# The order of the matmuls within a tile of an expert layer on one core: three whole passes in place of three products at each piece of weights

## The reference

```python
shared = jax.nn.silu(flat @ shared_gate_w) * (flat @ shared_up_w) @ shared_down_w
xs = flat[sorted_tok]                                # the two best of 16 experts for each token
g = jax.lax.ragged_dot(xs, gate_w, group_sizes)      # 1024 -> 512 per expert
u = jax.lax.ragged_dot(xs, up_w, group_sizes)        # 1024 -> 512
h = jax.nn.silu(g) * u
dn = jax.lax.ragged_dot(h, down_w, group_sizes)      # 512 -> 1024
routed = jnp.zeros_like(flat).at[sorted_tok].add(sorted_w[:, None] * dn)
output = (shared + routed).reshape(b, s, d)
```

## Time and profile before

| what | value |
|---|---|
| time, median of 3 runs | 3263.84 us (3263.45 to 3267.43) |
| the profiled execution's own time | 3260.97 us |
| its span, from first to last instruction | 3259.4 us |
| mean granted clock of TensorE | 0.974 |
| TensorE busy with matmuls | 3012.4 us, 92% |
| ScalarE, VectorE busy | 1025.7 us (31%), 1681.5 us (52%) |

### The profile page before, as it was taken

How to read it: one execution, slowest core, us unless ns; L and a number is a source line. 1 busy time by engine, 2 the same in 40 slices (tenths; PEclk the granted TensorE clock), 3 DMA queues, 4 the chain that set the end, 5 groups by cost and what they waited for, 6 DMA issues and landing times.

```text
span 3259.4 us, 50815 instructions
## 1 busy us (share of the span) xinstructions
PE 3012.4 (92%) x17478; PEld 2478.7 (76%) x17479; DVE 1681.5 (52%) x3164; ACT 1025.7 (31%) x1940; POOL 609.4 (19%) x572
## 2 busy tenths in 40 slices
PE   3799998898989998689999999999999999999998
PEld 3677777777777776578888888888888888888886
DVE  3687777787878775323333333333333334444444
ACT  3444443343444331223233333333333321111110
POOL 1233333333333432100000000000000001111111
PEclk9699999999999997799999999999999999999999
DMA  4333333333434321553333442443242234444444
GB/s 151 117 105 121 115 119 116 105 105 107 126 108 123 111 85 46 216 179 140 135 136 135 142 173 103 174 161 114 101 175 100 109 135 152 145 154 137 157 146 133
DMA packets 200706, 424.54 MB, mean 130 GB/s; under 512 B 85472, under 2 KB 85984, under 8 KB 200160
## 3 DMA queue, kind: packets, MB, share of 16 engines
q1 hardware_dynamic: 176160, 349.67, 31.8%
q0 software_dynamic: 24400, 72.96, 6.8%
HBM read 333.42 MB, written 102.27 MB: 134 GB/s over the span
## 4 chain that ended last, share of the span: by engine, by line
PE 54%; DMA 1%; DVE 1%; issue 1%; ACT 1%; SPq 1%; ACTq 0%; POOL 0%; POOLq 0%; DVEq 0%
PE p_g_b L1451 17%; PE p_up_b L1451 17%; PE p_y_b L1439 16%; PE p_x_b L1419 3%; PE p_h_b L1426 1%; DMA mid_y<-y_b 1%; DVE w_lo_b L1294 1%; ACT w_hi_b L1237 1%; SPq L1139 0%; DMA xg_b<-mid_xn,idx_b 0%; DMA r_b<-mid_y,slot_now_b 0%; ACTq L1103 0%; DMA idx_b<-mid_lists 0%; SPq L1138 0%; DVE r_b L1347 0%
## 5 line engine op out<-in xcount | busy, mean ns | idle before, releaser
L1310 DVE TENSOR_TENSOR ht_lo_b<-p_h_b,ht_hi_b 128x512 fp32r<-128x512 f32 x105 | 72.5, 691 | 557.4 <-ACT ht_hi_b L1249 553.4
L1451 PE MATMUL p_g_b<-w_hi_b,xt_hi_b 128*128 128x512 f32 x840 | 339.2, 404 | 20.3 <-DVE w_lo_b L1294 18.4
L1439 PE MATMUL p_y_b<-w_hi_b,ht_hi_b 128*128 128x512 f32 x840 | 336.9, 401 | 6.8 <-DVE ht_lo_b L1310 6.8
L1451 PE MATMUL p_g_b<-w_hi_b,xt_lo_b 128*128 128x512 f32 x840 | 328.9, 391 | 0.0
L1451 PE MATMUL p_up_b<-w_lo_b,xt_hi_b 128*128 128x512 f32 x840 | 328.7, 391 | 0.0
L1451 PE MATMUL p_up_b<-w_hi_b,xt_lo_b 128*128 128x512 f32 x840 | 328.5, 391 | 0.0
L1439 PE MATMUL p_y_b<-w_hi_b,ht_lo_b 128*128 128x512 f32 x840 | 328.1, 391 | 0.0
L1451 PE MATMUL p_up_b<-w_hi_b,xt_hi_b 128*128 128x512 f32 x840 | 328.0, 391 | 0.0
L1439 PE MATMUL p_y_b<-w_lo_b,ht_hi_b 128*128 128x512 f32 x840 | 327.9, 390 | 0.0
L1451 PE MATMUL p_g_b<-w_lo_b,xt_hi_b 128*128 128x512 f32 x840 | 326.8, 389 | 0.0
L1322 DVE SCALAR_TENSOR_TENSOR sg_b<-th_b,p_g_b 128x512 f32<-128x512 f32 x105 | 72.2, 687 | 486.6 <-ACT th_b L1279 486.6
(11 more groups left out here) (216 smaller groups left out, 5837.5 us busy)
## 6 DMA issues: line engine op xcount, KB each, us to landing
mid_y<-y_b SPq DMA_DIRECT2D x73, 512.0 KB, 3.3
x<-in_x SPq DMA_DIRECT2D x64, 512.0 KB, 3.7
gbd<-mid_g_row SPq DMA_DIRECT2D x64, 512.0 KB, 5.1
stage_b<-in_eg SPq DMA_DIRECT2D x16, 2048.0 KB
stage_b<-in_eu SPq DMA_DIRECT2D x16, 2048.0 KB, 15.2
stage_b<-in_ed SPq DMA_DIRECT2D x16, 2048.0 KB, 19.4
ctx_t<-in_ctx_t SPq DMA_DIRECT2D x32, 512.0 KB, 4.6
ctx_v<-in_ctx SPq DMA_DIRECT2D x32, 512.0 KB, 7.7
```

Source lines behind the costliest of these rows:

```text
L1310: nc.vector.tensor_tensor(ht_lo[:, :, :], p_h[:, :, :], ht_hi[:, :, :].bitcast(f32), ALU.subtract).then_inc(ht_rdy, 1)
L1439: last = nc.tensor.matmul(p_y[n][:, :], a[:, k, :], b[:, GUP + k, w], start=(k == 0 and m == 0), stop=(k == FE // P - 1 and m == 2))
L1451: mm = nc.tensor.matmul(out[:, :], a[:, k, :], w[:, k, o:o + FE], start=(k == 0 and m == 0), stop=(k == KD - 1 and m == 2))
```

## The change

In `body` and in `down` on TensorE, the loop over the three products is now outside of the loop over the pieces. A tile makes all its high by high products, then all low by high, then all high by low. Each pass waits only for the parts that it reads: the first for `xt_hi` (`xt_hi_rdy`) and `w_hi` (`gu_hi`), the second for `xt_lo` (`xt_rdy`) and `w_hi`, the third for `w_lo` (`gu_split`). In `down` likewise `d_hi` twice and `d_split`. `turn_h` is called behind piece 3 of the second pass. No other engine's program is changed.

```diff
-            trio = ((xt_hi, w_hi), (xt_lo, w_hi), (xt_hi, w_lo))
+            trio = ((xt_hi, w_hi, xt_hi_rdy, gu_hi), (xt_lo, w_hi, xt_rdy, gu_hi), (xt_hi, w_lo, xt_rdy, gu_split))
...
                 for n in range(2):
-                    for k in range(FE // P):
-                        if n == 0:
-                            pe.wait_ge(d_split, (PIECES - GUP) * e + (k + 1))
-                        w = slice(512 * n, 512 * n + 512)
-                        for m, (a, b) in enumerate(((ht_hi, w_hi), (ht_lo, w_hi), (ht_hi, w_lo))):
+                    w = slice(512 * n, 512 * n + 512)
+                    for m, (a, b, w_part) in enumerate(((ht_hi, w_hi, d_hi), (ht_lo, w_hi, d_hi), (ht_hi, w_lo, d_split))):
+                        for k in range(FE // P):
+                            if n == 0:
+                                pe.wait_ge(w_part, (PIECES - GUP) * e + (k + 1))
                             last = nc.tensor.matmul(p_y[n][:, :], a[:, k, :], b[:, GUP + k, w],
                                                     start=(k == 0 and m == 0), stop=(k == FE // P - 1 and m == 2))
                     last.then_inc(y_ps, 1)
 
             def body(i, q, e, c, first, prev, last):
                 ge(pe, h_rdy, i)
-                for k in range(KD):
-                    if k % 4 == 0:
-                        pe.wait_ge(xt_rdy, 2 * i + (k // 4 + 1))
-                    pe.wait_ge(gu_split, GUP * e + (k + 1))
-                    for m, (a, w) in enumerate(trio):
+                for m, (a, w, x_part, w_part) in enumerate(trio):
+                    for k in range(KD):
+                        if k % 4 == 0:
+                            pe.wait_ge(x_part, 2 * i + (k // 4 + 1))
+                        pe.wait_ge(w_part, GUP * e + (k + 1))
                         for out, o in ((p_g, 0), (p_up, FE)):
                             mm = nc.tensor.matmul(out[:, :], a[:, k, :], w[:, k, o:o + FE],
                                                   start=(k == 0 and m == 0), stop=(k == KD - 1 and m == 2))
-                    if k == 3 and prev:
-                        turn_h(i)
+                        if k == 3 and m == 1 and prev:
+                            turn_h(i)
```

## The result

| | before | after |
|---|---|---|
| time, median of 5 runs | 3263.45 us | 3300.41 us |
| span of the profiled execution | 3259.4 us | 3298.2 us |
| mean granted clock of TensorE | 0.974 | 0.969 |

The change makes the kernel 1.1% slower: the ratio is 1.0111, with a 95% interval from 1.0097 to 1.0125. By the ratio that is 36.2 us (31.7 to 40.8). The forecast was 3299 us, 35.2 us more than before. (The median before is 3263.45 us here, of five executions, and was 3263.84 us of three.)

What follows compares the result with a forecast made beforehand. TensorE's instruction stream was taken to bound the kernel. Fifteen switches at plus 2.21 us and one at 2.04 gave 35.2 us, all else nothing: 3263.84 + 35.2 = 3299 us, own range -6/+8, with 80% and more in 3290 to 3316.

Steps and rivals of the forecast that it cites:

- Bound: Expert part after the first expert: TensorE's instruction stream bounds it, busy 1247.96 of 1262.80 us; spacing and holes count.
- The old hole is filled: At a switch of weights, TensorE begins at about 1845.71 in place of 1846.82, filling a hole of 1.11 us.
- Pass one at the pace of the copies: At a switch, high by high follows ScalarE's copies, 0.951 us a piece against 0.453; net plus 2.21 us, 35.2 in all.
- Size of the wait in the profile: TensorE's waits for `w_hi`: 3 to 3.5 us a switch, some 50 in all, less by the modelled ends.
- First tile: First tile of the first expert: end at 1362.63 against 1362.60, no change.
- Down, `xt_hi_rdy`, added waits at nothing: Down in passes, `xt_hi_rdy` for the first pass, and 42 waits a tile in place of 14: each taken as costing nothing.
- What is late next: At a switch `turn_h` comes 2.2 us later; `ht_lo`, the next gather and SP's loads add nothing.
- No slack: TensorE after 1424.80: no slack to take up the loss but 15 and 13 us, mostly switch holes; no-change rival 2%.
- The clock rival: TensorE's clock falls during high by high at switches: 26 us more, 3325 us; chance 7%.
- The faster rival: Only the first `w_lo` held TensorE up at switches, so 18 us would go: 3246 us; chance 3%.

Runs made afterwards that it cites:

- finer waits: Kernel before with its order kept; each piece's first gate-up product waits for the copy, the third for the subtraction: ratio 0.9936.
- early copies: ScalarE makes its eight copies ahead of taking out the left half of y: against the kernel before, ratio 0.9933; with the whole change added, 0.9956 (3247.69 us).
- down alone: Only the down product in three passes, gate and up piece by piece as in the kernel before: ratio 0.9996.
- the kernel with the old waits: The change's three passes, but every pass waits for the low parts (`gu_split`, in down `d_split`), against the kernel before: ratio 1.0242.

## Why the prediction was right, point by point

- *Bound.* Right: TensorE's stream sets the expert part, and a hole on it is time.
- *The old hole is filled.* Right: no idle between 1860.02's four matmuls and 1860.93, as forecast, and alone it is worth 0.91 us a switch (finer waits) to 1.26 (early copies, 18.97 to 17.71).
- *Pass one at the pace of the copies.* Right, to the hundredth: 7.05 us forecast and measured, 0.06 hand-over, copies 0.95 apart. 2.21 us a switch forecast, 2.19 measured (21.16 less 18.97); 2.04 and 2.02 at the last; 35.2 in all, 34.9 measured over the 16. That the median came within 2 us of 3299 is in part luck, since its interval is some 4.5 us wide to either side; what bears the forecast out is the agreement switch by switch.
- *Size of the wait in the profile.* The sentence on "some 50 in all (less by the modelled ends)" was loose: the waits view shows 25.7. It counts idle from modelled ends; by the starts it is 3.42 us a switch.
- *First tile.* Right in the main: 18.56 us from its transposes to the next, 18.49 before. But this one tile took 18.01 to 18.07 us in three other kernels whose first tile has the order and waits of before, where TensorE's clock rose 0.9 to 1.2 us sooner behind the first product. So its single length can show a change only from some 0.5 us on.
- *Down, `xt_hi_rdy`, added waits at nothing.* Right: down alone changes nothing, and the steady tiles, with 28 more waits each, keep 17.71 us. With 0.02 us a pass boundary a steady tile would be 0.12 us longer.
- *What is late next.* Right: `turn_h` and its split came later, and the down product behind them did not wait.
- *No slack.* The reading of the earlier trace rows was half wrong. The 15 us of idle in the expert part are mostly the holes at the switches. The 13 us behind 2687.60 are not: from there to 3210 TensorE was busy throughout, and all of them lie in the last 49.4 us (36.47 us busy), at the end of the kernel. It changes nothing in the forecast, since no slack lay where the loss arose.
- *The clock rival.* Rightly held unlikely for this kernel (1.00 in pass one), but near: it happened in the kernel with the old waits, where the idle is 0.40 in place of 0.21 us. The prediction weighed it against the right rows. The rule of the Trainium skill that the prediction set beside them ("TensorE: Matmul & The Clock Gate", A second HAM failure mode: psum-queue depth-cycling) is that very short idles between groups of matmuls, if frequent enough, make the clock swing. It fits what the kernel with the old waits showed, and not what this change showed.
- *The faster rival.* Its condition was copies ahead of pass one; early copies went most of that way, and the three passes then came out faster than before.
- *Beyond the sum.* The span grew by 38.8 and not 35.2: beside the 34.9, 2.4 us are the first stage, 0.3 less come behind the last transposes, and 1.9 are the first five tiles, where a long wait for the store of y lies. The kernel with only gate and up in passes took 99.1 us for these five, so I take them as no part of the change.

## What to carry to other kernels

When a consumer starts on pieces while a producer still makes them, compare the work per piece with the time per piece: an order that waits for less can still lose if it uses up each piece faster than the next one comes. Do at a piece all that its parts allow, and relax the wait inside that order; and before reordering the consumer, look whether the producer can simply start sooner, here by 2.7 us (4.0 ahead of TensorE in place of 1.3). Measure such an effect by the distance of starts in the tiles concerned; waits by modelled ends showed less than half of it.

## What the runs showed of the hardware that I had not expected

- Waits that were already satisfied cost TensorE nothing here: with 28 more in each, the steady tiles stayed at 17.71 us. Few of them are instructions of their own: the trace has 51235 instructions against 50815 before, which is 4 more for each of the 105 tiles and not 28.
- The granted clock came out differently in two kernels that differ little. Two matmuls every 0.95 us, with 0.21 idle between pairs, kept 1.00 at all 16 switches. Two every 1.14 us, with 0.40 idle and behind a hole of 0.70 to 0.97, lost it at 6 of 16, and these six tiles have a mean clock of 0.86 or 0.93; four of them took 24.4 to 25.3 us in place of 23.74. In the other two it fell and came back while pass one was still held by its waits, and cost nothing. The runs don't show which of the differences (the idle, the hole ahead, the longer pass) decides, nor why 10 of the 16 alike switches kept the clock.
